# A fused decoder layer with routed experts on one Trainium2 core: the first attention's queries and keys projected for two batches at a time, a new order of steps, and no identity products among the last routing steps

## The reference

```
# 1. one-head attention over the rows, then layer norm
Q = x @ W1 + b1;  K = x @ W2 + b2;  V = x @ W3 + b3
out = softmax(Q @ K.T / 16) @ V @ W4 + b4
x = _ln(x + out)
# 2. a post-norm block: 16-head cross attention to ctx (8, 375, 256) with a mask,
#    16-head self attention, a feed-forward layer 256 -> 1024 -> 256 with gelu,
#    each with residual, norm, gain and shift;  x = _ln(x + block(x))
# 3. routed experts, 8 of them, one for each row
expert = argmax(x @ centroids.T);  alpha = sigmoid(x . centroids[expert])
h = ln(x) * gamma[e] + beta[e]
y = x + relu(h @ W1[e].T + b1[e]) @ W2[e].T + b2[e]
x = _ln(x + alpha * y + (1 - alpha) * x)
```

## Time and profile before

| | us |
|---|---|
| median of 3 runs (418.32 to 419.86) | 419.78 |
| the profiled execution | 419.55 |
| its span | 417.8 |
| TensorE busy | 396.3 |
| VectorE busy | 272.9 |
| ScalarE busy | 237.7 |
| GpSimd busy | 129.9 |

### The profile page before, as it was taken

The page is one execution under the profiler, slowest core; times in us unless marked ns, Lnnn a source line. Parts: engine busy times, 40 slices in busy tenths (PEclk is TensorE's granted clock), DMA queues, the critical chain, the costliest instruction groups (busy, mean ns, idle before and its releaser), DMA issues.

```text
span 417.8 us, 10554 instructions
## 1 busy us (share of the span) xinstructions
PE 396.3 (95%) x3750; PEld 331.7 (79%) x3750; DVE 272.9 (65%) x940; ACT 237.7 (57%) x810; POOL 129.9 (31%) x258
## 2 busy tenths in 40 slices
PE   8989999999999999999999999999999999999980
PEld 7757887878888778788787888887888888999560
DVE  5577676777677777686775833758778776335420
ACT  1104785698787787888879978764412132423220
POOL 5251024114014123031230313315453545833221
PEclk9999999999999999999999999999999999999996
DMA  7970170510010104200000004950194422599000
GB/s 214 276 224 19 36 213 21 219 38 18 2 31 25 40 2 159 99 9 11 2 2 2 4 1 167 428 212 3 36 417 188 143 74 84 201 418 382 30 28 18
DMA packets 11417, 46.97 MB, mean 112 GB/s; under 512 B 1552, under 2 KB 6128, under 8 KB 9200
## 3 DMA queue, kind: packets, MB, share of 16 engines
q1 hardware_dynamic: 8896, 31.79, 21.7%
q0 software_dynamic: 1920, 12.35, 7.7%
q10 hardware_dynamic: 544, 2.08, 1.7%
HBM read 41.31 MB, written 4.91 MB: 111 GB/s over the span
## 4 chain that ended last, share of the span: by engine, by line
PE 62%; DVE 7%; ACT 5%; issue 1%; POOL 1%; DVEq 0%; POOLq 0%; ACTq 0%
PE bank_pt L737 9%; PE bank_scores L600 7%; PE bank_out L611 7%; PE bank_pt L772 6%; PE bank_out L585 5%; PE bank_out L759 5%; PE bank_out L571 5%; PE bank_out L782 4%; PE bank_scores L721 3%; PE bank_out L578 3%; ACT arena L1317 2%; ACT arena L1328 2%; PE bank_scores L727 1%; ACT arena L1337 1%; DVE arena L1067 1%
## 5 line engine op out<-in xcount | busy, mean ns | idle before, releaser
L1337 ACT ACTIVATE arena<-bank_pt 125x448 f32<-125x448 f32 (+1 forms) x128 | 66.1, 546 | 37.7 <-PE bank_pt L737 36.1
L1317 ACT ACTIVATE arena<-arena,negmaxc 112x375 f32<-112x375 f32 x128 | 76.5, 603 | 13.6 <-DVE negmaxc L1067 13.6
L1067 DVE CUSTOM_DVE_ANT_0 arena<-bank_scores,arena 112x375 f32<-112x375 f32 x128 | 64.7, 541 | 17.9 <-PE bank_scores L727 12.5
L737 PE MATMUL bank_pt<-ident,arena 112*125 112x112 f32 (+1 forms) x512 | 74.3, 276 | 1.4 <-ACT arena L1337 0.8
L737 PEld LDWEIGHTS bank_pt<-ident,arena 112*125 112x125 f32 (+1 forms) x512 | 63.2, 175 | 13.5 <-ACT arena L1337 3.4
L585 PE MATMUL bank_out<-arena 128*112 128x256 f32 (+1 forms) x224 | 56.2, 384 | 0.1
L1423 POOL TENSOR_TENSOR vareps<-meanvar,scal 112x1 f32<-112x1 f32 (+1 forms) x49 | 10.2, 209 | 134.0 <-DVE meanvar L946 124.2
L1328 ACT ACTIVATE arena<-bank_scores,negmaxs 112x112 f32<-112x112 f32 x128 | 43.2, 353 | 4.3 <-DVE negmaxs L1073 4.0
L585 PEld LDWEIGHTS bank_out<-arena 128*112 128x112 f32 (+1 forms) x224 | 37.9, 181 | 8.9 <-issue 2.1
L1376 ACT ACTIVATE arena<-bank_scores,consts 128x128 f32<-128x128 f32 x64 | 18.2, 368 | 40.7 <-PE bank_scores L600 40.7
L571 PE MATMUL bank_out<-arena 128*128 128x112 f32 x320 | 40.2, 277 | 0.1
(11 more groups left out here) (186 smaller groups left out, 667.7 us busy)
## 6 DMA issues: line engine op xcount, KB each, us to landing
arena<-moe SPq DMA_DIRECT2D x8, 2048.0 KB, 12.9
arena<-ctxT SPq DMA_DIRECT2D x8, 375.0 KB, 3.4
arena<-mask SPq DMA_DIRECT2D x8, 164.1 KB, 3.1
x_slots<-arena SPq DMA_DIRECT2D x8, 130.0 KB, 2.7
arena<-x_slots SPq DMA_DIRECT2D x8, 130.0 KB, 2.2
arena<-weights SPq DMA_DIRECT2D x1, 1024.0 KB, 5.0
arena<-fi SPq DMA_DIRECT2D x1, 1024.0 KB, 6.0
arena<-fo SPq DMA_DIRECT2D x1, 1024.0 KB, 8.3
```

Source lines behind the costliest of these rows:

```text
L737: last = nc.tensor.transpose(dst[0:kp, j * S:(j + 1) * S], probs[0:S, (n % 2) * HG + j, c * kp:(c + 1) * kp], ident[0:S, 0:S])
L1067: v.tensor_tensor_reduce(out=probsC[0:S, i % (2 * HG)], in0=score_bank[j][0:S, 0:KX], in1=masks[0:S, u % 2], scale=-1.0, scalar=3.0e38, op ...
L1317: a.activation(probsC[0:S, i % (2 * HG)], probsC[0:S, i % (2 * HG)], ACT.Exp, bias=negmax["c"][0:S, u, at:at + 1], scale=-1.0, accum_out=s ...
L1337: a.activation(probsT[0:kp, n % RT, c], pt_bank[PT[stage, i] % RP][0:kp, 0:HG * S], ACT.Copy).then_inc(pt_free, 1)
```

## The change

Three things are changed. From batch 2 on, queries and keys are projected for batches 2 and 3, 4 and 5, 6 and 7 together, with 224 columns in each product; batches 0 and 1 stay single. VectorE's three evictions (two for the queries, one for the keys) are 224, 224 and 448 columns wide. `QTa` and `KTa` hold two pairs instead of two batches and lie in the memory that the feed-forward layer's hidden values use later. The steps have a new order, by new starts, lags and corrections. `WARM` is empty, so the 27 identity products are gone, and the totals and the first expert's chunks are due later.

The table `SHIFT` has some 370 entries, most of them changed; one line of it is shown. The rest of the diff is nearly whole.

```diff
-FIRST_START = (-1.72, -1.29, 0.03, 1.76, 8.93, 13.57, 13.97, 19.52)
-FIRST = {"aw": -6.16, "aqk": -8.92, "av": -6.28, "as": -8.17, "at": -6.64, "ay": -5.8, "ab": -2.61, "ax": -1.48}
+FIRST_START = (-1.72, -1.29, 0.07, 1.77, 8.94, 13.57, 13.99, 19.52)
+FIRST = {"aw": -6.4, "aqk": -8.92, "av": -6.28, "as": -8.17, "at": -6.64, "ay": -5.8, "ab": -2.61, "ax": -1.49}
...
-SHIFT = {("zx", 0): 0.03, ("aqk", 0): 0.05, ("aw", 0): -0.72, ("at", 0): -0.34, ("av", 0): 0.46, ("ab", 0): -1.5,
+SHIFT = {("zx", 0): 0.03, ("aqk", 0): -0.43, ("aw", 0): -1.13, ("at", 0): 0.09, ("av", 0): 0.46, ("ab", 0): -1.94,
...
-WARM = {("f2", 7): 5, ("sc", 6): 5, ("rk", 6): 4, ("zx", 7): 6, ("ei", 0): 3, ("rk", 7): 4}
+WARM = {}
 WARM_FIRST = 6
-HEAD = {"en": (0.21,), "ei": (-0.28,), "first": (0.41, 0.45, 0.46, 0.47, 0.48, 0.49, 0.5, 0.51), "tot": (0.39,)}
-SEND = (41.63, 44.43, 46.78, 50.45, 50.94, 53.52, 55.79, 57.94)
+HEAD = {"en": (1.01,), "ei": (-0.03,), "first": (0.66, 0.67, 0.7, 0.73, 0.75, 0.84, 1.06, 2.07), "tot": (0.64,)}
+SEND = (41.49, 44.39, 46.98, 50.42, 51.68, 53.69, 57.74, 57.9)
+
+def aqk_of(u):
+    return u if u < 2 else u - u % 2
+
+def batches_of_aqk(u):
+    return [u] if u < 2 else [u, u + 1]
...
+    order = [step for step in order if step[0] != "aqk" or aqk_of(step[1]) == step[1]]
...
-        QTa, KTa = ring(C * S, rows_T), ring(C * S, rows_T)
...
+        pairs = hiddenT.rearrange("p r f n -> p (r f n)")[:, 0:8 * C * S]
+        QTa, KTa = [pairs[:, t * 4 * C * S:(t + 1) * 4 * C * S].rearrange("p (r c s) -> p r c s", r=2, c=C) for t in range(2)]
+        assert 8 * C * S + 2 * XW <= 2 * FC * FN
...
+                    n = len(batches_of_aqk(i))
                     for q, w in enumerate(("W1", "W2")):
                         if i == 0 and q == 1:
                             pe.wait_ge(w_second, 16)
-                        project_T(slot + q, W[w], xT_sb[:, i])
+                        dst = out_slot(slot + q)
+                        for m in range(C):
+                            for k in range(C):
+                                last = mm(dst[:, m * n * S:(m + 1) * n * S].rearrange("p (b s) -> p b s", b=n), W[w][:, k, m * 128:(m + 1) * 128],
+                                          xT_sb[:, i:i + n, k], start=k == 0, stop=k == C - 1)
+                        last.then_inc(out_full, 1)
...
-                    pe.wait_ge(out_free, OUT["aqk", i] + 2)
+                    pe.wait_ge(out_free, OUT["aqk", aqk_of(i)] + 2)
+                    at = slice(i % 2 * S, (i % 2 + 1) * S)
...
-                        last = mm(dst[0:S, 0:S], QTa[:, i % 2, k], KTa[:, i % 2, k], start=k == 0, stop=k == C - 1)
+                        last = mm(dst[0:S, 0:S], QTa[:, i // 2 % 2, k, at], KTa[:, i // 2 % 2, k, at], start=k == 0, stop=k == C - 1)
...
-                    if i >= 2:
-                        dve.wait_ge(pt_full, PT["as", i - 2] + 1)
+                    n = len(batches_of_aqk(i))
+                    at = slice(i % 2 * S, (i % 2 + n) * S)
+                    if i >= 4:
+                        dve.wait_ge(pt_full, PT["as", i - 3] + 1)
```

More of the change, by code:

```diff
@@ L64 @@
+CONTEXT_START = (0.46, 1.73, 7.28, 13.14, 16.14, 19.64, 23.59, 27.64)
+CONTEXT = {"ck": (-1.95, -1.57), "cv": (-1.19, 0.57, 1.02)}
 LAG = 8
-CROSS = {"cq": (-1.05,), "cy": (5.68,), "cb": (6.18,), "cx": (6.84,)}
+CROSS = {"cq": (-1.05,), "cy": (5.68,), "cb": (6.17,), "cx": (6.89,)}
 SCORES = -0.15
-HEADS = (-0.1, -0.09, 0.01, 0.14)
+HEADS = (-0.11, -0.1, 0.01, 0.14)
 CROSS_GROUP = {"ct": (0.78, 1.46, 1.89)}
-PAIR = {"cn": 1.85, "sn": 2.51, "pr": 3, "pv": 3.22}
+PAIR = {"cn": 1.85, "sn": 2.57, "pr": 3, "pv": 3.22}
@@ L950, in _ @@
                 if stage == "aqk":
-                    if i >= 2:
-                        dve.wait_ge(pt_full, PT["as", i - 2] + 1)
+                    n = len(batches_of_aqk(i))
+                    at = slice(i % 2 * S, (i % 2 + n) * S)
+                    if i >= 4:
+                        dve.wait_ge(pt_full, PT["as", i - 3] + 1)
                     src = full(slot)
                     for m in range(C):
-                        last = v.tensor_scalar(QTa[:, i % 2, m], src[:, m * S:(m + 1) * S], col("b1", m), 1.0 / D ** 0.5, ALU.add, ALU.mult)
+                        last = v.tensor_scalar(QTa[:, i // 2 % 2, m, at], src[:, m * n * S:(m + 1) * n * S], col("b1", m), 1.0 / D ** 0.5, ALU.add, ALU.mult)
                     last.then_inc(out_free, 1)
-                    add_bias(KTa[:, i % 2], full(slot + 1), "b2").then_inc(out_free, 1)
+                    v.tensor_tensor(KTa[:, i // 2 % 2, :, at], full(slot + 1)[:, 0:C * n * S].rearrange("p (c s) -> p c s", c=C),
+                                    consts[:, COLS["b2"]:COLS["b2"] + C].unsqueeze(2).to_broadcast([128, C, n * S]), ALU.add).then_inc(out_free, 1)
                 elif stage in ("cq", "sqk"):
```

10 lines of the change are left out of this document (4 added, 6 removed), and 125 rows, old and new, of the table SHIFT.

## The result

The changed kernel took 415.74 us (median of 5 runs, 412.96 to 416.87) beside 418.99 us for the kernel before (5 runs, 418.32 to 419.86). The medians lie 3.25 us apart. The ratio that the measurement gives, which isn't the quotient of the two medians, and which is used from here on, is 0.9886: about 4.8 us less, with a 95% interval of 0.9838 to 0.9935, or 6.8 to 2.7 us. The profiled execution took 412.96 us, the quickest of its five, so the two profiles lie further apart (6.6 us of span) than either figure says.

The account below looks back on a forecast made before the run. TensorE, busy 396.3 of 417.8 us, was taken as the bound. Terms -0.85 (pairs), -1.3 (first 30 us), 0, 0 and -0.9 (last steps) sum to -3.05: 419.55 becomes 416.5, median 416.6, range 414.3 to 419.8 us.

Parts of the forecast that it names:

- is untouched by the change: Very end, the last tile's normalisation and scatter: claimed not to be affected, so no term was priced there.
- 24 x 0.467 = 11.21 us: Query and key projections: price of 24 products with 224 columns, replacing 48 products costing 12.05 us.
- 1.2 us earlier: Last routing steps: VectorE's arg-max work for batch 6 done at 329.95 instead of 331.16; 1.0 us of it taken.
- The pairs: Query and key projections of batches 2 to 7 on TensorE: 0.85 us less, ends 0.4 and 1.3 us.
- The first 30 us: Start of the kernel: early key projections cover three TensorE waits, 1.3 us less; ends 1.8 saved, 0.5 lost.
- no idle over 0.3 us: Sign that the forecast is right: no TensorE idle time above 0.3 us between 23 and 29 us.
- The other moves in the middle: Steps reordered among independent ones in the middle: taken as 0, ends 2.0 us less and 2.0 us more.
- The low clock at 290 to 296 us: Slow feed-forward records there lose 1.65 us: left at 0; rival that it vanishes gives 414.9 us, chance 0.16.
- The last steps and the first tile: Last routing steps and first expert's layers: 0.9 us less, with the clock falling to half for 3.4 us.
- VectorE can go on at about 328.5: Last routing steps: batch 6's scores come ahead of batch 7's second layer, so VectorE need not wait until 329.71.
- no fall: Rival, last steps: clock stays full, 2.2 us less in place of 0.9, total 415.3 us; chance 0.12.
- low clock lasts: Rival, slower: 1.2 GHz through both layers of the first expert, +4.7 us in place of -0.9, total 422.1; chance 0.09.

Follow-up runs that it names:

- experiment 3: Kernel before with queries and keys by pairs only, its order of steps and identity products kept; ratio 1.0026.
- experiment 7: Changed kernel's order without identity products, but single projections instead of pairs; ratio to the kernel before 0.9958.
- experiment 6: Changed kernel plus 27 identity products that never run, in the skipped block of the last expert tile; ratio to the kernel before 0.9945.
- experiment 8: Kernel before with pairs and the new order up to scores 16, then the old order and identity products; ratio 0.9966.
- experiment 9: Changed kernel unaltered, measured again on another chip; ratio to the kernel before 0.9908.
- experiment 11: Changed kernel plus 23 never executed identity products in the last expert tile's block; ratio to the kernel before 0.9917.
- experiment 1: Kernel before with its identity products removed and nothing else changed; ratio 1.0022.
- experiment 4: Kernel before with only the last steps in the new order, single projections, no identity products; ratio 0.9961.
- experiment 12: Pairs in the old order, without the four identity products behind the last ranking; ratio to the kernel before 1.0007.
- experiment 2: Changed kernel with the 27 old identity products put back; ratio to the kernel before 0.9887.
- experiment 5: Changed kernel with 18 identity products only where TensorE waits; 412.97 us, ratio to the kernel before 0.9833.
- experiment 10: Changed kernel with the 18 identity products in the waits, run again beside the changed kernel; 416.17 us, ratio to the kernel before 0.983.

## Why the prediction came out as it did

I forecast 3.05 us less, and faster is what came. The ratio says 4.8 us less, the medians 3.25, the interval 2.7 to 6.8, so the total by itself can't show how far the size was off. The parts can, and they say that the total came near by errors of both signs. By size the first step that failed is the sentence that the very end "is untouched by the change": a term left at nothing, which measured 2.77 us. The second is the price of the pairs, "24 x 0.467 = 11.21 us". The third is VectorE's chain in the last steps, "1.2 us earlier". That the sum wasn't further out is luck.

**The pairs: the size was off.** The price came from a group whose mean held the slow records of the earlier trace rows; at full clock the product costs 0.408 us, and 12.05 less 9.8 is 2.25 us, not 0.85. The row of full-clock products was among my rows: 1.68 us for 8 records is 0.42 us a product, and I didn't use it. My upper end of 1.3 us excluded the truth. What I had not seen at all is that this gain is only there if the order moves with it: no gain in the old order (experiment 3), 0.5 to 0.7% in the new (the changed kernel against experiment 7).

**The first 30 us: right in size, not in its reason.** The scores start 1.41 us earlier (forecast 1.3), but only 0.4 us of that is idle time between 23 and 29 us; my sign "no idle over 0.3 us" failed three times. One of the three pairs, batches 2 and 3, is projected here: 16 products of 0.251 become 8 of 0.408, 0.75 us, which I had booked elsewhere. So the waits gave a third of what I said, and 0.26 us I can't place. The start of the scores also differs between runs of one order: 30.69 to 31.36 us in the new one (the changed kernel, experiments 6, 8, 9, 11) and 32.10 to 33.21 in the old (before, 1, 3, 4, 12), but 32.51 to 36.14 where TensorE waited for one of the first transfers (2, 5, 7, 10).

**The other moves in the middle: taken as 0.** From scores 0 to ranking 0 the profile gives 1.71 us less, and the two pairs that lie there account for 2.25 - 0.75 = 1.5 of it; so 0 was right, as far as pairs and order can be parted. Experiments 3, 7 and 8 say that they can't: the order's worth is to keep the pairs' gain.

**The low clock at 290 to 296 us: left at 0, gone in this profile.** It is no effect of the order. Of the 14 profiles eight have it (before and experiments 2 to 6, 10 and 11) and six don't; experiments 3 and 12 have one order up to there, and one has it. With the same instructions up to there, experiments 5, 6, 10 and 11 have it and the changed kernel and experiment 9 don't. It made 1.65 us of the difference between the two profiles, and says nothing of the change.

**The last steps and the first tile: 0.9 us forecast, nothing found.** The step that failed is "VectorE can go on at about 328.5", and with it the 1.2 us. It counted what batch 6's scores gain by standing ahead and not what batch 7's second layer loses behind them. In experiment 4 that layer starts 0.67 us later, the last normalisation comes 0.69 us earlier, and behind it the small products at half clock take most of the rest: the chain from it to the slot takes 6.59 us where it took 6.05, so 0.15 us is left. The clock fell as said. The price of the fall was about right there (1.6 us against 1.7); in the changed kernel the fall starts at 325.6 us and lasts to 335.8, and the two layers of the first tile take 9.4 us in place of 7.28: 2.1 us lost. With the same instructions it is 1.8 us in experiment 6 and 2.8 in experiment 9. Experiments 5 and 10 show what the fall costs as a whole: the same order with the waits filled has no fall in these steps, and is 2.0 and 2.3 us shorter from ranking 7 to tile 1. The rivals "no fall" and "low clock lasts" were both wrong; without a fall the new order with filled waits is worth 1.5 to 1.7 us (experiments 10 and 5), not 2.2.

**The end: not priced.** I wrote that the end is untouched by the change. Its instructions are, but it is 2.77 us shorter, the largest difference in the table. In all 14 profiles the end is long where the program has at most 24 TensorE products fewer than before (before, experiments 2, 3, 6, 8) and short where it has 27 or more fewer (the changed kernel, 1, 4, 5, 7, 9 to 12). Experiments 6 and 11 part it from everything that runs. Without it the total of the changed kernel would be about that of experiment 6: 0.9945, 2.3 us less than before (1.0 to 3.6). The forecast's 3.05 lies in this interval and in that of the changed kernel, so the totals can't say which of the two it met; it was made for the first.

What makes the end long can be seen in the traces. Behind its last product TensorE's own instruction stream (PEldq in the views) still passes over the blocks of the tiles that these inputs don't use: eight branches, or ten before, and then a DRAIN and a last EVENT_SEMAPHORE. The branches (L492) and the closing pair (L251), count and then shortest, median and longest in ns and the first and last start in us, of the changed kernel and then of experiment 6 (one of the nine branches lies ahead of the last product):

```profile
L492 PEldq COMPARE_BRANCH  x9: 208/208/2734, 401.4 to 410.7; - x9
L251 PEldq DRAIN  x1: 8/8/8, 411.0 to 411.0; - x1
L251 PEldq EVENT_SEMAPHORE  x1: 51/51/51, 411.2 to 411.2; - x1
```

```profile
L492 PEldq COMPARE_BRANCH  x9: 208/208/2792, 403.1 to 412.5; - x9
L251 PEldq DRAIN  x1: 8/8/8, 412.8 to 412.8; - x1
L251 PEldq EVENT_SEMAPHORE  x1: 51/51/51, 416.0 to 416.0; - x1
```

Most branches take 0.21 us, but a few stop for 2.4 to 3.1 us. The changed kernel has two such stops, at 404.95 and 408.22, and its closing pair follows at once. Experiment 6 has two as well, and a third of 3.3 us between the DRAIN and the last semaphore, with all other engines done since 412.9. The nine profiles with a short end have two stops each; the five with a long one have three, the third being a branch (before, 2.35 us) or the gap ahead of the last semaphore (2, 3, 6 and 8, 2.5 to 3.3 us).

Each of these stops goes with one read of instructions. Traffic from 400 us on, in slices of 0.5 us, of the changed kernel and then of experiment 6; a lone 33 is one 16 KB packet of the instruction queue, and 254 is the last scatter:

```profile
GB/s 262 16 0 33 0 0 0 0 0 49 0 0 16 0 254 8 33 0 0 0 0 0 33 0 0 0 0 0 0 0 0 0 0 0 0 0 0 0 0 0
```

```profile
GB/s 0 0 0 123 139 16 33 0 0 0 0 0 0 49 0 0 16 8 254 33 0 0 0 0 0 0 33 0 0 0 0 0 0 0 0 0 0 0 0 0
```

The packets come 3 to 3.5 us apart. In these two profiles and in that of before, each stop ends 2.3 to 2.8 us after the start of such a packet. In the changed kernel the last packet, at 411.4, is one that nothing waits for. In experiment 6 TensorE's last instruction, at 416.04, comes 2.8 us behind the packet of 413.2. That TensorE has a third stop where the end is long is shown. That each stop is a wait for a block of TensorE's own code, and that the length of the program sets how many such waits fall into the end, is inferred from this order in time and from experiments 6 and 11; the trace doesn't name the engine that a packet is for.

## What to carry to other kernels

Price a product by records at full clock, not by the mean of a group that holds slow ones. When a step moves ahead of another, count also what the other loses. Don't put down to an edit what a single profile may or may not have, like the low clock at 290 us. Where TensorE waits for short chains ahead of dense work, put in identity products that fill the waits and delay nothing, rather than many or none: here that is worth 0.5 to 0.8%, in intervals that overlap a little, and 2.0 to 2.3 us in the profiles. And look at the time between the last work and the end of the span: it can depend on how long the program is, so a comparison of two kernels should say whether it moved, and an edit should be judged without it.

## What was unexpected of the hardware

- The end of the program is a step in its length: 27 products that never run add 3.1 us behind TensorE's last product (12.29 against 9.21), 23 add none (9.01). Branches over skipped blocks take 0.21 us, or 2.4 to 3.1 us where the stream stops.
- The granted clock of 0.90 in 324 to 326 us puts the fall at 325.6, at the end of a wait of 2.00 us, and the 0.54 in 334 to 336 its end at 335.8: 10.2 us at 1.2 GHz, the last 4 of them dense work. In experiments 6 and 11, with the same instructions, the fall lasts 6.8 us, and in the one that I had to go by it was 3.4. A single fall is no bound for another.
- 24 products of 224 columns in place of 48 of 112 save 19% of their time, and the same saving is worth nothing in one order of steps and 0.5 to 0.7% of the kernel in another.
- In experiments 9, 10 and 11 ScalarE stood for 3.02 to 3.72 us ahead of an activation with its input ready for most of that time, and the tiles took 3.2 to 5.7 us longer; open.
